# One table of count and weight pairs for the dense adjacency of a graph kernel, its weights turned to source order by TensorE

## What is computed

```python
def reference(x, src, dst, edge_attr_5, edge_weight, ...):
    x = x + L0(relu(layernorm(x)))   # counts
    x = x + L1(relu(layernorm(x)))   # weights, three times
    x = x + L2(relu(layernorm(x)))   # a gather, no sum over edges
    x = x + L3(relu(layernorm(x)))   # counts, times an attention value
    return x

# L0: messages = bn_relu(concat(h[src], edge_rep[dst]) @ W1)
#     edge_new = segment_sum(messages, dst)
#     aggregate = segment_sum(edge_new[dst], src)
#     out = bn_relu(bn_relu((h + aggregate) @ W2a) @ W2b)
# L1: deg = segment_sum(w, dst);  norm = dinv[src] * w * dinv[dst]
#     three times: agg = segment_sum(out[src] * norm, dst)
#                  out = out + relu((0.1 * agg + 0.9 * x0) @ conv_w[i])
# L3: out = segment_sum(sigmoid(a1[src] + a2[dst]) * xj[dst], src) + h
```

## Time and profile before

| | us |
|---|---|
| median of 3 runs | 3560.21 (3559.28 to 3560.83) |
| span of the profiled execution | 3565.2 |
| first column added to `counts` | 144.06 |
| z stage | 549.0 to 1378.8 |
| message stage | 1416.5 to 1815.9 |
| pass 0 | 1963.8 to 2186.6 |
| last column added to `weights` | 2354.44 |
| pass 1 | 2371.8 to 2592.8 |
| passes 2 and 3 | 2614.4 to 2844.5, 2866.1 to 3094.0 |
| pass 4 | 3329.7 to 3549.8 |

### The profile page before, as it was taken

The page is one execution under the profiler, slowest core; times in us unless marked ns, Lnnn a source line. Parts: engine busy times, 40 slices in busy tenths (PEclk is TensorE's granted clock), DMA queues, the critical chain, the costliest instruction groups (busy, mean ns, idle before and its releaser), DMA issues. The chain is left out here.

```text
span 3565.2 us, 41686 instructions
## 1 busy us (share of the span) xinstructions
PE 2424.9 (68%) x12339; PEld 1976.6 (55%) x12339; DVE 2395.4 (67%) x4693; ACT 1352.5 (38%) x2800; POOL 1734.6 (49%) x1269
## 2 busy tenths in 40 slices
PE   4668733454555543666621999879999999925998
PEld 3522213454444443444421897469888988923788
DVE  5979945777777778877886544344565566615788
ACT  2268833444444441000000435424434434423776
POOL 0257887776667667888888777730000000042000
PEclk9779865555555555888855999889999999966999
DMA  9993224665555656555533774146545645340355
GB/s 373 351 355 34 22 26 130 174 171 164 165 165 166 172 170 137 133 142 134 143 40 39 202 177 89 1 103 185 175 126 172 185 130 173 118 103 8 109 173 176
DMA packets 338453, 517.84 MB, mean 145 GB/s; under 512 B 145379, under 2 KB 227100, under 8 KB 331580
## 3 DMA queue, kind: packets, MB, share of 16 engines
q1 hardware_dynamic: 190254, 436.41, 38.2%
q0 software_dynamic: 134768, 58.41, 14.2%
q10 hardware_dynamic: 13214, 20.35, 1.7%
HBM read 369.65 MB, written 145.38 MB: 144 GB/s over the span
## 5 line engine op out<-in xcount | busy, mean ns | idle before, releaser
L1133 PE MATMUL banks<-rows_r,lhs_r 128*128 128x448 f32 x3500 | 899.1, 372 | 84.0 <-issue 41.6
L728 POOL DMA_INDIRECT counts<-wts x391 | 637.4, 1630 | 307.9 <-DMA counts<-ring 141.0
L1133 PEld LDWEIGHTS banks<-rows_r,lhs_r 128*128 128x128 f32 x3500 | 667.8, 191 | 152.9 <-issue 74.8
L741 POOL DMA_INDIRECT weights<-wts x391 | 620.9, 1588 | 161.8 <-issue 159.1
L1133 PE MATMUL banks<-ring_r,lhs_r 128*128 128x448 f32 x1750 | 525.8, 370 | 0.0
L749 POOL DMA_INDIRECT reg<-tab_p,w x416 | 406.9, 978 | 217.9 <-issue 122.8
L548 DVE SCALAR_TENSOR_TENSOR ring_r<-ring,dinv,rows_r 128x896 fp32r<-128x896 f32 (+1 forms) x300 | 303.7, 1033 | 309.5 <-ACT rows_r L535 309.3
L1221 PE MATMUL banks<-lhs_r,oT 128*128 x416 | 203.3, 489 | 429.8 <-issue 346.6
L535 ACT ACTIVATE rows_r<-ring,dinv 128x896 fp32r<-128x896 f32 (+1 forms) x300 | 285.0, 951 | 399.3 <-PE banks L1133 342.0
L799 POOL DMA_INDIRECT el<-tab_l,base_i x25 | 24.0, 958 | 796.8 <-DMA tab_l<-reg 789.5
L1221 PEld LDWEIGHTS banks<-lhs_r,oT 128*128 128x128 f32 x416 | 131.9, 317 | 447.3 <-issue 447.0
(11 more groups left out here) (269 smaller groups left out, 4104.6 us busy)
## 6 DMA issues: line engine op xcount, KB each, us to landing
ring<-weights SPq DMA_DIRECT2D x225, 448.0 KB
ring<-counts SPq DMA_DIRECT2D x150, 448.0 KB
zbuf<-reg SPq DMA_DIRECT2D x208, 256.0 KB
reg<-zbuf SPq DMA_DIRECT2D x52, 1024.0 KB
counts<-ring SPq DMA_DIRECT2D x25, 1568.0 KB, 16.4
weights<-ring SPq DMA_DIRECT2D x25, 1568.0 KB
ring<-weights SPq DMA_DIRECT2D x75, 224.0 KB
dr<-low_rows_d SPq DMA_DIRECT2D x52, 256.0 KB
```

Source lines behind the costliest of these rows:

```text
L728: pool.indirect_dma_start(counts, bass.IndirectOffsetOnAxis(ap=ix_c[:, k:k + 1], axis=0), vals_c[:, k:k + 1], None, compute_op=ALU.add).th ...
L741: pool.indirect_dma_start(weights, bass.IndirectOffsetOnAxis(ap=ix_w[:, k:k + 1], axis=0), vals_w[:, k:k + 1], None, compute_op=ALU.add).t ...
L1133: m = pe.matmul(bank[:, 0:BLK], lhs[part], rows[:, c:c + BLK], start=first, stop=last)
```

## The change

There is one table, `pairs`, with a row for each destination and a column for each source, whose cells are 8 bytes: the count and the weight. POOL adds 391 columns to it, each an indirect DMA of 128 elements of 8 bytes (`add_cell`), where there were two times 391 of 4 bytes. The pair tests, their loads on SP, and the second set of cell numbers (`t_wc`, `ix_w`) are gone. SP zeroes `pairs` with 25 DMAs of 3136 KB, and POOL waits for all of them before its first add. POOL's order is now 133 columns, the 416 gathers with one column after every eighth, and then 206 columns, with the wait for the group before at every seventh column.

`weights` still exists, by source, and passes 1 to 3 read it as before. It is now written during pass 0. There the ring brings pairs, so the weights pass through SBUF as well: PE transposes the weight half of each unit (`turn`, four transposes into PSUM), ACT copies it out of PSUM (`turn_out`) into one of two buffers `turned`, each for the two row tiles of a pair, and SP stores a pair as 448 rows of 1 KB (`store_turned`, two DMAs), after the load of a later unit. A unit of pass 0 is one block: 175 units of 128x448 pairs, in the groups ((0, 3), (3, 3), (6, 1)), since two banks (6 and 7) now belong to the transposes. ACT may only write a buffer of `turned` again when its store has landed.

In pass 4 the ring brings pairs too, 128x896 of them for a two-block unit, in 3 slots of twice the width in place of 6. A slot is free when `count_att` has read it; the product goes to `att` and its low part to `att_low`, no longer into the ring.

```diff
 GROUPS = ((0, 4), (4, 3))
+GROUPS_0 = ((0, 3), (3, 3), (6, 1))
...
+C_FIRST = 19 * NG
+C_EVERY = 8
+TURN_LAG = 1
+TURN_LEAD = 2
...
+            wide = zeros.unsqueeze(1).to_broadcast([P, 2 * NB, BLK])
+            for t in range(NT):
+                sp.dma_start(pairs_rows[t * P:(t + 1) * P].rearrange("r (a b) -> r a b", a=2 * NB), wide).then_inc(zeroed, 16)
...
-            pool.wait_ge(zeroed_c, 16 * (NT + 1))
-            add_counts(W_FROM)
-            pool.wait_ge(zeroed_w, 16 * (NT + 1))
-            while done_c < C_FIRST:
-                add_counts(NG)
-                add_weights(W_PER)
+            pool.wait_ge(zeroed, 16 * (NT + 2))
+            for k in range(C_FIRST):
+                add_cell(k)
...
             for k in range(KS):
                 gather(k)
-                if k % 4 == 3:
-                    add_counts(C_PER)
...
+                if k % C_EVERY == C_EVERY - 1:
+                    add_cell(done)
+                    done += 1
+            for k in range(done, NE):
+                add_cell(k)
...
+            def add_cell(k):
+                if k % NG == 0:
+                    pool.wait_ge(cells_ready, k // NG + 1)
+                    wait(pool, cell_added, 16 * k)
+                    pool.sem_inc(pool_go, 1)
+                pool.indirect_dma_start(pairs, bass.IndirectOffsetOnAxis(ap=ix_c[:, k:k + 1], axis=0),
+                                        vals[:, k, :], None, compute_op=ALU.add).then_inc(cell_added, 16)
...
+            def store_turned(q):
+                _, _, t, (b,) = UNITS[q]
+                if t % 2 == 0 and t < NT - 1:
+                    return
+                k, c0 = turn_slot(q), t // 2 * 2 * P
+                n = min(2 * P, LD - c0)
+                sp.wait_ge(drained_a, nth[number["turn", (q,)]])
+                sp.dma_start(weights_rows[b * BLK:b * BLK + 3 * P, c0:c0 + n].rearrange("(i p) c -> p i c", p=P),
+                             turned[k][:, 0:3, 0:n]).then_inc(turn_stored[k], 16)
+                sp.dma_start(weights_rows[b * BLK + 3 * P:(b + 1) * BLK, c0:c0 + n],
+                             turned[k][0:BLK - 3 * P, 3, 0:n]).then_inc(turn_stored[k], 16)
...
                     load_unit(q)
+                    if pi == 0 and q >= RING + TURN_LAG:
+                        store_turned(q - RING - TURN_LAG)
...
+            def turn_out(q):
+                t, k = UNITS[q][2], turn_slot(q)
+                if t % 2 == 0:
+                    wait(act, turn_stored[k], 32 * (pair_no[q] // 2))
+                bank = empty_bank(act, number["turn", (q,)])
+                n = min(P, LD - t * P)
+                emptied(act.activation(turned[k][:, :, t % 2 * P:t % 2 * P + n],
+                                       bank.rearrange("p (i c) -> p i c", i=4)[:, :, 0:n], ACT.Copy))
...
+            for q in range(FIRST[1]):
...
                 high_rows(q)
+                if q >= TURN_LEAD:
+                    turn_out(q - TURN_LEAD)
...
+            def turn(q):
+                _, full, n = ring_slot(q)
+                pe.wait_ge(full, n)
+                bank = open_bank(number["turn", (q,)])
+                for i, (o, w) in enumerate(W3):
+                    m = pe.transpose(bank[0:w, i * P:(i + 1) * P], counted(q)[:, o:o + w, 1], ident[:, :])
+                m.then_inc(filled, 1)
```

More of the change, by code:

```diff
@@ L88 @@
 ZS, SQ = 8, 4
[L89 to L98, removed]
+C_FIRST = 19 * NG
+C_EVERY = 8
+TURN_LAG = 1
+TURN_LEAD = 2
+W3 = ((0, P), (P, P), (2 * P, P), (3 * P, BLK - 3 * P))
 class Signal:
@@ L138, in psum_plan @@
     pairs = [(g,) for g in range(-(-NT // 2))]
-    dense = [key for gi in range(len(GROUPS)) for key in group_keys(gi)]
+    dense = [[key for gi in range(len(groups_of(pi))) for key in group_keys(pi, gi)] for pi in range(5)]
     plan = []
@@ L151, in psum_plan @@
     add("mean", [(0,), (1,)], "V")
-    add("agg0", dense, "V")
+    add("turn", [(0,)], "A")
+    for q in range(FIRST[1]):
+        if q + 1 < FIRST[1]:
+            add("turn", [(q + 1,)], "A")
+        if UNITS[q][2] == NT - 1:
+            add("agg0", unit_keys(q), "V")
     add("h2", [(j, b) for j in range(2 * JH) for b in range(NB)], "A")
@@ L160, in psum_plan @@
     for li in range(3):
-        add(f"agg1{li}", dense, "V")
+        add(f"agg1{li}", dense[1 + li], "V")
         add(f"cv{li}", pairs, "V")
@@ L171, in psum_plan @@
     add("a1", [(b,) for b in range(NB)], "A")
-    add("agg3", dense, "V")
+    add("agg3", dense[4], "V")
     add("back3", pairs, "V")
@@ L330, in gnn_kernel @@
         att = [view(RD + k * UW, UW) for k in range(ROWS)]
+        att_low = [rounded(f"att_low{k}", RD + k * UW, UW) for k in range(ROWS)]
+        turned = [view(RF + k * 8 * P, 4, 2 * P) for k in range(2)]
+        assert 16 * P <= DR
         outT = view(RC, JH, NP)
@@ L640, in load_unit @@
             def load_unit(q):
[L641 to L647 removed]
+                pi, _, t, blocks = UNITS[q]
+                slot, full, _ = ring_slot(q)
@@ L663, in _ @@
+            sp.wait_ge(cell_added, 16 * NE)
             for q in range(RING):
@@ L955, in _ @@
                 high_rows(q)
+                if q >= TURN_LEAD:
+                    turn_out(q - TURN_LEAD)
+            for q in range(FIRST[1] - TURN_LEAD, FIRST[1]):
+                turn_out(q)
             for stage, dest, nj in (("h2", h2T, 2 * JH), ("h3", h3T, JH)):
@@ L1109, in back @@
                     m.then_inc(filled, 1)
-            def dense(pi):
-                name = passes[pi]
-                for q in range(pi * PU, (pi + 1) * PU):
-                    _, gi, t, h = unit(q)
-                    blocks = unit_blocks(gi, h)
-                    if gi == 0 and h == 0:
+            def turn(q):
[5 more added lines that the diff above has]
+                m.then_inc(filled, 1)
+            def dense(pi):
+                name = PASSES[pi]
+                if pi == 0:
+                    turn(0)
+                for q in range(FIRST[pi], FIRST[pi + 1]):
+                    if q + 1 < FIRST[1]:
+                        turn(q + 1)
+                    _, gi, t, blocks = UNITS[q]
+                    if gi == 0 and blocks[0] == 0:
                         if pi == 1:
```

352 lines of the change are left out of this document (155 added, 197 removed).

## The result

The changed kernel takes 3701.55 us in the median of 4 runs (3690.83 to 3713.66), the kernel before in the same sets 3560.52 (3559.28 to 3567.05). The ratio is 1.0394, with a 95% interval of 1.0373 to 1.0415: slower, as forecast, but by 141 us where 76 were forecast, and 1.6 us over the upper end of the range. The profiled execution has a span of 3688.8 us, 123.6 over the one before. The profiled execution of the changed kernel was the shortest of its four (3690.83), so the table accounts for 124 of the 141 us.

What follows compares the result with a forecast made beforehand. It took table waits, PE in the dense passes, and PE and DVE in the z stage as bounds. Terms -137 + 220 - 10 + 3 = +76 turned the 3565.2 us span into 3641, forecast 3636 us, range 3518 to 3700.

Steps and rivals of the forecast that it cites:

- Sign and mechanism of pass 0: Pass 0: a loop through two turned buffers, SP's order and PE sets the pass, making it +220 us longer.
- the rival without it (3521): Pass 0: the store loop does not bind, DMA sets the pass, +105 in place of +220, 3521 us; chance 0.16.
- Its size: Pass 0: loop of 10.0 us for four units, 443 us in place of 222.8, +220.
- The upper bound of 503: Pass 0: slow bound, a loop of 11.4 us with dearer transposes and PE at 0.83, 503 us, +280.
- z stage: Between the first and last gather: 52 adds in place of 104 gain nothing, since POOL waits for DVE there.
- the second of the rivals: z stage: POOL was its bound, so 52 adds fewer give up to 100 us, 3536 us; chance 0.07.
- Front and adds after the gathers: POOL's adds before and after the gathers: 1.85 us each, group waits of 2.1 and 2.3; first gather at 542, -3 us.
- Start of pass 0: Pass 0 starts at 1827 in place of 1963.83, -137 us, with POOL's path later than DVE's.
- Pass 1: Start of pass 1: no more wait for weights, dinv on DVE is late next, -10 us (0 to -11).
- Pass 4: Pass 4: two-block units of 917 KB take 2.5 us against 2.48 on PE, +3 us (0 to +15).
- The rival on transposes and the clock: Pass 0: transposes do not hold PE's clock, PE alone needs 588 us, +145, 3781 us; chance 0.04.
- Eight bytes at the price of four: POOL's adds: count decides, not bytes; the rival had 8-byte adds cost twice, +525, 4160 us; chance 0.04.

Runs made afterwards that it cites:

- e1: The changed kernel with TURN_LAG 0 in place of 1, so each pair's store in pass 0 stands one ring load earlier: 3581.25 us, ratio 1.0083.
- e2: The changed kernel with TURN_LAG -1 in place of 1, so a pair's store waits for the use of unit 2p only: 3542.46 us, ratio 0.9974.
- e4: The changed kernel with an add after every fourth gather in place of every eighth (104 adds in the z stage): 3712.89 us, ratio 1.0439.
- e8: The kernel before, without the pair table, with an add to counts after every eighth gather in place of every fourth: 3653.22 us, ratio 1.0276.
- e7: The changed kernel with no adds between the gathers and 258 after them: 3790.98 us, one run.
- e5: The changed kernel with four ring slots (wide, narrow, wide, narrow) for pass 4's second group in place of three wide ones: 3678.19 us, ratio 1.0346.
- e3: The changed kernel without the stores of the turned weights and the waits for them, transposes and copies kept: 3499.84 us, one run.

## Why the prediction was right and wrong

**Sign and mechanism of pass 0: right.** The loop of two buffers, SP's order and PE was last, and the rival without it (3521) did not come. e1 and e2 showed it by moving the store alone. **Its size: wrong by 68 us.** The loop was 11.7 in the mean, 12.0 in the round shown, and not 10.0, and two of its terms were too small: the step that failed in pass 0. The landing of the store, with the load ahead of it, was put at 1.2 + 3.05 = 4.25; it was 5.34 in the round shown, from the issue of the store's second DMA (64 KB) behind the first (384 KB), whose own median from issue to landing is 4.8:

```profile
weights<-reg SPq DMA_DIRECT2D x84, 384.0 KB, 4.8
```

The 3.6 us for 650 KB came from a stage with little else on the queues (81 to 136 GB/s over it). And PE's part was put at 3.7 with a clock of 0.9; in the round shown it was 5.0 (1.10, 2.23, 0.45 and 1.24). The two halves of it do the same work: 3.33 us after the gap and 1.69 after that. The message stage had shown as much: 5.38 and 5.24 after gaps of 3.81 and 2.38. I took the middle between "stays up" and "falls" for a gap of 2.9, though 2.38 had fallen already. The hand-overs came to 0.3 in all, 0.6 less than I took, and the issues of the load and the store to 0.75, 0.2 more; I had left out that of the store. So the 2.0 us are 1.1 for the landing and 1.3 for PE, less 0.4. The upper bound of 503 was too low for the same reason: it had no higher price for the landing.

**z stage: the step that failed in kind.** I priced 52 fewer adds at nothing, because POOL waited 94.3 us for DVE, and gave the other case, the second of the rivals (called the third where the stage is priced), 0.07. The stage became 76 us shorter, three quarters of that rival's 100, and by e4 and e8 the adds make 62 to 80 of it. That POOL waits for DVE in some passes does not keep it from being late in others; in the waits of the z stage of the kernel before stands a row that I passed over, and e8 has it too, with half the adds (us, times, longest):

```profile
DVE reg L1599 <- remote: 103.2, 27, 11.0
```

```profile
DVE reg L1599 <- remote: 50.1, 16, 6.2
```

L1599 is the instruction that reads the gathered rows. That these waits are for gathers is only argued, since the profile names no DMA there and the instruction also waits for a store of earlier results; e7, with no adds at all, still has 47.2 us of them. That taking adds out shortens the stage is shown. Since the gain stood against the loss in pass 0, it hid 76 us of the error there: that the time came within 1.6 us of the range is luck.

**Front and adds after the gathers: 20 us each too low.** I knew that the waits between groups would no longer be covered, and took 2.1 and 2.3 us for them. The 2.3 was called the middle of 2.08 and 3.53, rounded down; the middle is 2.8, and with it the 29 groups would have been 14 us nearer. What was measured for each group is 3.0, made up of 2.3 and 2.5 us of waiting beyond the 0.30 and of longer adds and other gaps, for which the sum had no term. The zeros were 3.6 us later.

**Start of pass 0.** POOL's path was last, as said: on DVE `edge_new` was done at 1760.8, 27 us before pass 0. The pair tests had to go for that all the same. They stood for 114 us between the message stage and `edge_new` (1815.9 to 1929.64 before), and with them DVE would have been last, by an estimate from these rows. From the last add to the first products it was 11.3 and not 14.5.

**Pass 1: right**, -13 for -10. **Pass 4: +22 for +3**, outside its bound of 15. I compared a unit's bytes with a unit's products and looked only at the mean; the first group lost 2.7 us and the second 19.5. In the second a wide and a narrow unit take turns in three slots of one size, and a wide load took 6.8 us in the median there, which three slots did not cover. e5 gave back 16 of the 22.

**The rival on transposes and the clock: rightly given little.** "TensorE: Matmul & The Clock Gate", Part 4, of the Trainium skill says that a transpose doesn't count as PE-busy in the same way as a product. e3 had the 700 transposes among products with a clock of 0.99, and in the kernel before the clock came back from 0.52 to 1.00 within 50 transposes in a row (this window, then the last of the earlier trace rows). So the traces do not agree with the page.

```profile
2281.00:2284.40 3.40, 3.40 (x18) 3.23 (x17) 2.56 (x5) 3.32 (x6) 2.79 (x3) 0.52 0.25 5
```

This chip's transposes of 128x128 float32 took 0.11 us each in a row (0.45 for four).

**Eight bytes at the price of four: right.** 1.55 us of issue for an add in both kernels (1.60 in the mean, for 1.63 before).

## What to carry to other kernels

When work is handed round between engines through a small number of buffers, write the round down as one list of links and move each link to the earliest place where its own condition allows: here one number that moved a store by two loads was worth 152 us, more than any engine's load in that stage suggested. In this loop each gap of 2.4 to 3.6 us on TensorE was paid twice, once as the gap and once as products at half the clock behind it; and the place of an instruction on an issuing queue was a wait like any other. And an engine that waits for another in some passes may still set the pace in others, so taking work off it should be priced by a run, or at least with a range, and not at zero. Work that is only moved behind the stage is not saved, as e8 shows.

## What the runs showed of the hardware

An indirect add of 128 elements of 8 bytes takes POOL as long to issue as one of 4 bytes, 1.55 us. With stores of 1 KB pieces beside the ring loads the mixture moved 333 to 338 GB/s at a DMA share of 0.98, where loads alone showed 370 in a window of 3.3 us and 364 over the 130 us of pass 4's first group; whether it is the size of the pieces or that they are written, no run tells. After a gap of 2.65 us on PE, the same four transposes and six products took 3.33 us at a granted clock of 0.52, and 1.69 at 1.00.
